# A twelve-sublayer decoder on one core: the delta-rule layer's join, its decay weighting, the latent copy order and one table of decays

## What is computed

```python
scores = jnp.einsum('bhsr,bhlr->bhsl', q_r, k_r)
attn = jax.nn.softmax(scores, axis=-1)
ctx_c = jnp.einsum('bhsl,bld->bhsd', attn, kv_rope)
```

```python
fused_qkv = jax.nn.silu(conv_out)          # causal convolution, 4 taps, over 4096 channels
def step(Sm, inp):
    q_t, k_t, v_t, b_t, a_t = inp
    Sm = Sm * a_t[..., None, None]
    kv = jnp.einsum('bhk,bhkv->bhv', k_t, Sm)
    u = (v_t - kv) * b_t[..., None]
    Sm = Sm + k_t[..., None] * u[:, :, None, :]
    o = jnp.einsum('bhk,bhkv->bhv', q_t, Sm)
    return (Sm, o)
```

## Time and profile before

| | |
|---|---|
| median of 3 runs | 2896.03 us (2892.81 to 2896.42) |
| the profiled execution: own time | 2889.24 us |
| its span | 2887.4 us |
| PE busy | 2364.2 us (82%) |
| DVE busy | 1698.7 us (59%) |
| ACT busy | 1015.2 us (35%) |
| POOL busy | 769.9 us (27%) |

### The profile page before, as it was taken

One profiled execution on the slowest core, in us unless ns is written; L12 is line 12 of the kernel. 1 busy time (PEld: TensorE's weight loads), 2 busy tenths in 40 slices (PEclk: granted clock), 3 DMA queues, 4 the chain that ended last, 5 costly groups with the idle time before them and its releaser, 6 DMA issues. The chain is left out here.

```text
span 2887.4 us, 38148 instructions
## 1 busy us (share of the span) xinstructions
PE 2364.2 (82%) x14562; PEld 1587.5 (55%) x14562; DVE 1698.7 (59%) x3527; ACT 1015.2 (35%) x2336; POOL 769.9 (27%) x573
## 2 busy tenths in 40 slices
PE   6797453348999988878889797889998888999899
PEld 4555322114345555657768586745558665555555
DVE  5435986893445652496969687436656753656311
ACT  3132021651035541135444353435552132555210
POOL 1130001000048862110101010028880000888222
PEclk8689555559999999987979797899999958999999
DMA  1000001002000010220101010210001003000411
GB/s 36 19 21 23 0 0 20 1 23 88 0 1 1 1 51 9 107 57 16 44 16 44 16 45 16 51 52 1 1 1 44 21 6 97 1 1 1 121 38 40
DMA packets 100526, 81.77 MB, mean 28 GB/s; under 512 B 52704, under 2 KB 91857, under 8 KB 99770
## 3 DMA queue, kind: packets, MB, share of 16 engines
q1 hardware_dynamic: 99321, 77.89, 9.5%
q0 software_dynamic: 1024, 1.45, 0.2%
HBM read 73.58 MB, written 5.35 MB: 27 GB/s over the span
## 5 line engine op out<-in xcount | busy, mean ns | idle before, releaser
L2032 POOL TENSOR_SCALAR work<-work,small 128x512 f32<-128x512 f32 x384 | 594.3, 1566 | 706.6 <-DVE small L1967 705.3
L2010 ACT ACTIVATE work<-psum,small 128x512 f32<-128x512 f32 x384 | 260.6, 683 | 254.6 <-DVE small L1962 254.6
L1962 DVE TENSOR_REDUCE small<-psum 128x2 f32<-128x1024 f32 x192 | 234.7, 1224 | 176.0 <-PE psum L1912 176.0
L1922 PEld LDWEIGHTS psum<-consts,work 128*128 128x128 f32 x1536 | 165.5, 141 | 114.0 <-issue 101.8
L1912 PE MATMUL psum<-keysT,arena_a 64*128 64x512 f32 x768 | 219.2, 649 | 8.9 <-ACT work L2010 6.0
L1934 PE MATMUL psum<-work,keys 128*64 128x256 f32 x1536 | 187.0, 384 | 36.6 <-issue 34.2
L1922 PE MATMUL psum<-consts,work 128*128 128x128 f32 x1536 | 211.4, 281 | 3.6 <-DVE work L1973 2.6
L1934 PEld LDWEIGHTS psum<-work,keys 128*64 128x64 f32 x1536 | 120.0, 136 | 136.5 <-issue 110.5
L2864 PE MATMUL psum<-xnT,arena_a 128*128 128x256 f32 x512 | 137.4, 423 | 25.8 <-DVE arena_b L3284 23.8
L1973 DVE COPY work<-psum 128x512 f32<-128x512 f32 x192 | 130.9, 682 | 19.7 <-PE psum L1922 19.5
L2017 ACT ACTIVATE work<-psum 128x512 f32<-128x512 f32 x192 | 114.4, 596 | 71.5 <-PE psum L1922 71.5
(11 more groups left out here) (585 smaller groups left out, 4777.6 us busy)
## 6 DMA issues: line engine op xcount, KB each, us to landing
arena_b<-alpha_rows SPq DMA_DIRECT2D x16, 512.0 KB, 5.7
arena_a<-in_L_xattn_Wo SPq DMA_DIRECT2D x3, 2048.0 KB, 13.6
arena_a<-in_L_xattn_Wq SPq DMA_DIRECT2D x3, 2048.0 KB, 13.7
arena_a<-in_L_xattn_w_kc_q SPq DMA_DIRECT2D x3, 1536.0 KB, 12.8
arena_a<-in_L_attn_w_qkv SPq DMA_DIRECT2D x1, 4096.0 KB
arena_a<-in_L_xattn_W_qr SPq DMA_DIRECT2D x3, 768.0 KB
arena_b<-in_L_ffn_w_fc SPq DMA_DIRECT2D x1, 2048.0 KB
arena_b<-in_L_ffn_w_proj SPq DMA_DIRECT2D x1, 2048.0 KB
```

Source lines behind the costliest of these rows:

```text
L1922: mm = nc.tensor.transpose(ps[:, 4 + j, c * P:(c + 1) * P], probs[u % NPB][:, j, c * P:(c + 1) * P], k.c["ident"])
L1962: nc.vector.tensor_reduce(top[:, 2 * u:2 * u + 2], ps[:, u % 2 * 2:u % 2 * 2 + 2, :], AX.X, ALU.max, negate=True).then_inc(*maxed.up())
L2010: nc.scalar.activation(probs[u % NPB][:, j, :], ps[:, u % 2 * 2 + j, :], ACT.Exp, bias=top[:, i:i + 1], accum_out=total[:, i:i + 1]).then_ ...
L2032: nc.gpsimd.tensor_scalar(probs[u % NPB][:, j, :], probs[u % NPB][:, j, :], total[:, i:i + 1], None, ALU.mult).then_inc(*scaled.up())
```

## The change

It has four parts.

1. In the delta stage the last two value tiles, 14 and 15, are no longer convolved ahead of `turn_blocks` but inside the join: each ahead of one of the two `z1d` copies on DVE. They get a place of their own, `late` (the space of `X`), and tile 15 a bank of its own; their transpositions stand after `close_first` and after `second_level(0)` on PE, their silu and keep between the join's copies on ACT. The join's PSUM banks are packed into 0, 1, 6 and 7 (`join_bank`), and the waits for the kept values move from `close_first` to the products that read them.
2. For g = 2 and 3 the weighting in `lower` is split: ACT writes the key products times `gn` (`weigh_keys`, eight instructions for each g), DVE multiplies all four heads by the decays in one instruction. `lower(b, 3)` comes after `convolve(b, 4)`. ACT's root of the key norms comes after both.
3. In the latent stages ACT copies first and takes the exponentials second in even steps; odd steps stay as they were.
4. In `l0_attn` the exponential is that of half of the argument, and two of the three squarings go.

```diff
-            k.link(act, nc.scalar.activation(powers, arg, ACT.Exp, scale=0.125), "act")
+            k.link(act, nc.scalar.activation(powers, arg, ACT.Exp, scale=0.5), "act")
...
-            k.link(dve, nc.vector.tensor_tensor(powers, powers, powers, ALU.mult), "dve")
-            k.link(dve, nc.vector.tensor_tensor(powers, powers, powers, ALU.mult), "dve")
             dve.wait_ge(*low.at(1))
...
             for s in range(U + LAG):
+                if s % 2 == 0 and 0 <= s - LAG < U:
+                    keep(s - LAG)
                 if s < U:
                     exps(s)
-                if 0 <= s - LAG < U:
+                if s % 2 == 1 and 0 <= s - LAG < U:
                     keep(s - LAG)
...
+    late = over[:, 3072:4096].rearrange("p (n j s) -> p n j s", n=2, j=2)
...
+        if n < 8:
+            return qkT[:, 2 * pair(n):2 * pair(n) + 2, :]
+        return late[:, n - 14] if n >= 14 else vT[:, (n + 2) % 4]
+    def bank_of(n):
+        return 3 if n == 15 else n % 3
+    def join_bank(g):
+        return g if g < 2 else 4 + g
...
-                    pool.wait_ge(*vturned.at(8 * b + 6 + 2 * r))
+                    pool.wait_ge(*vturned.at(8 * b + 4 + 2 * r))
...
-                if n >= 3:
+                if n == 15:
+                    pe.wait_ge(*normed.at(2 * b + 2))
+                elif n >= 3:
                     pe.wait_ge(*conved.at(16 * b + n - 2))
...
-                for n in range(10, 16):
+                for n in range(10, 14):
                     turn_values(b, n)
                     if n < 13:
                         project(b, n + 3)
...
                 close_first(b, 1)
-                for g in range(5):
+                turn_values(b, 14)
+                second_level(b, 0)
+                turn_values(b, 15)
+                for g in range(1, 5):
                     second_level(b, g)
...
+            def weigh_keys(b, g):
+                act.wait_ge(*kkd.at(4 * b + g + 1))
+                if g == 2:
+                    act.wait_ge(*negated.at(b + 1))
+                    if b >= 1:
+                        act.wait_ge(*u1d.at(4 * b))
+                for j in range(2):
+                    for h in range(4 * g + 2 * j, 4 * g + 2 * j + 2):
+                        for c in range(2):
+                            last = nc.scalar.activation(inv[:, h, c * P:(c + 1) * P],
+                                                        ps[:, 4 + g, (2 * j + c) * P:(2 * j + c + 1) * P],
+                                                        ACT.Copy, scale=gn[:, c, h:h + 1])
+                last.then_inc(*weighed.up())
...
                 silu(b, 3)
+                weigh_keys(b, 2)
                 first_tap(b, 4)
-                act.wait_ge(*normed.at(2 * b + 1))
+                weigh_keys(b, 3)
...
             def lower(b, g):
+                if g >= 2:
+                    dve.wait_ge(*weighed.at(2 * b + g - 1))
+                    dve.wait_ge(*scanned.at(8 * b + 2 * g + 2))
+                    nc.vector.tensor_tensor(four(inv, g), four(inv, g), four(decay, g), ALU.mult).then_inc(*lmade.up())
+                    return
...
-                for g in range(4):
+                for g in range(3):
                     lower(b, g)
-                for n in range(4, 8):
+                convolve(b, 4)
+                lower(b, 3)
+                for n in range(5, 8):
                     convolve(b, n)
...
-                for n in range(10, 16):
+                for n in range(10, 14):
                     convolve(b, n)
 
                 turn_blocks(b, 0)
                 turn_blocks(b, 1)
                 for r in range(2):
+                    convolve(b, 14 + r)
                     dve.wait_ge(*z1d.at(2 * b + r + 1))
```

More of the change, by code:

```diff
@@ L2800, in dest @@
     def dest(n):
-        return qkT[:, 2 * pair(n):2 * pair(n) + 2, :] if n < 8 else vT[:, n % 4]
+        if n < 8:
[5 more added lines that the diff above has]
+        return g if g < 2 else 4 + g
     def four(t, g):
```

63 lines of the change are left out of this document (39 added, 24 removed).

## The result

The changed kernel takes 2825.68 us (median of 4 runs, 2822.46 to 2830.59), beside 2895.59 us for the kernel before on the same chip (4 runs, 2892.81 to 2896.42). The ratio is 0.9762, with a 95% interval of 0.9745 to 0.9779: 69 us less, between 64 and 74. The profiled execution took 2822.46 us, and its span is 2820.6 us. The forecast was 2829 us.

A forecast was written before the change was run, and what follows sets the result against it. PE bounds the latent stages, a chain over DVE and PE the delta stage. 39 us latent plus 4 x 6.9 us delta, 67 us off the 2896.0 us median, gave 2829 us, range 2820 to 2847 us.

The forecast's parts named there:

- Part 3, 39 us: Latent stages: with the copy first, PE's 87 waits of 0.45 us before `over_keys` go, 39 us.
- The slack: Latent stages: even-step exponentials start 0.35 us later, with 3 us of slack before the scores two steps on.
- POOL, next in line: Latent stages: POOL has 6.19 us of work in a pair, against 6.92 us; PE stays the bound.
- Part 1, 4.0 us a batch: Delta join: `close_first(1)` gains 5.1 us, less 0.9 and 0.2 for PE's transposes, 4.0 us a batch.
- that for POOL's clearing: Delta join: POOL's clearing keeps its distance to the transposes of tile 13; 0.3 us allowed.
- Part 2, 2.9 us a batch: Delta weighting: DVE saves 1.9 us net, plus 1.0 of the stop before the last `attend`, 2.9 us a batch.
- tile 4's earlier place: Delta, before the solve: tile 4 convolved some 2.9 us earlier starts PE's chain sooner, so 1.0 of the 1.15 us stop goes.
- Part 4, nothing: First layer: dropping two squarings gains nothing; DVE's idle time before its copy becomes 9.4 us instead of 4.24.
- The sum: Whole kernel: 39 + 4 x (4.0 + 2.9) = 66.6, say 67 us.
- PE's granted clock is 0.50, that is 1.2 GHz, throughout: Delta join: PE's clock stays at 1.2 GHz, even when busy for all of 6.00 us.
- PE at 0.50 in the join: Sign for part 1 in the delta join; the prediction is wrong if the clock rises there.
- The rival with the join at 2.4 GHz: Delta join straight after the projections runs at full clock: 8.4 us a batch, 34 us in all, 2795 us; chance 0.06.

The follow-up runs named there:

- The kernel with later tiles: The changed kernel with tile 14 convolved behind both first-level copies, tile 15 behind the first second-level copy; ratio 0.9682 to the kernel before.
- added products: The changed kernel with ten unused products of 128x128 by 512 columns in TensorE's waits of each join; ratio 0.9737 to the kernel before.

## Why the prediction was right

- *Part 3, 39 us.* 87 waits of 0.45 us were the right price: 3 x 13.3 = 39.9 us in the trace, and 39.9 us measured with that part alone, where the interval (35 to 45) makes so close a match chance. The slack was there too: a pause of 1.94 us in front of the exponentials leaves the pair at 6.91 us. POOL, next in line, stands still for 0.73 us in each pair.
- *Part 1, 4.0 us a batch.* The stretch from the solve to the second-level copy is 4.03 us shorter. Of the allowances, that for POOL's clearing was used (a stop of 0.25 us). In batch 1 0.3 us come back behind that copy: 0.12 in the second level, where I had put tile 15's transposes at 0.2, and 0.17 behind the join, unforecast. So 3.7 us are left. The terms inside held too: `close_first(1)` starts 5.1 us earlier, counted from the last step of the solve (22.95 instead of 28.05 us), as forecast, and tile 14's transposes cost 1.04 us ahead of the second level, where I had 0.9.
- *Part 2, 2.9 us a batch.* 3.10 us: the multiplications cost 1.13 us, as taken from the squaring, ScalarE's second group 2.23 us, tile 5's tap came 0.9 us early instead of 0.4, and the stop of 1.15 us went whole, where I had taken 1.0 of it. As to why it went: I named tile 4's earlier place. It gives TensorE's chain 1.13 us more cover, which alone would nearly have done it. Undone, it brings back only 0.45 us, since that chain is by then 0.70 us shorter than before; the granted clock was low for 3.4 us at its start instead of 6.8, which my sum didn't have. The join part isn't the reason, since alone it leaves a stop of 1.34 us.
- *Part 4, nothing.* 0.9995 with that part alone; the idle time is 9.46 us, forecast 9.4.
- *The sum.* 66.6 us forecast, 69 measured (64 to 74). The profiled executions differ by 66.8.
- *The step that failed, without a price.* "PE's granted clock is 0.50, that is 1.2 GHz, throughout", and with it "PE at 0.50 in the join" as the sign to look for. The row behind it began where the small products of before began, at 1478, and there it was true. In the changed kernel `join_first` begins 1.2 us behind the end of the last projection (1449.86 to 1451.08; before, 6.4 us, 1471.24 to 1477.60), and runs at 1.00 to its end. It takes 4.34 us instead of 7.04, and that gained nothing: VectorE, with tile 14 in front of the copy, came to it 7.1 us behind its first transposition, where 6.9 and an allowance of 0.3 were forecast. I wrote that the prediction would be wrong if the clock rose in the join. It was up in the first part of it, and the number held all the same, because TensorE was not what was waited for there. The kernel with later tiles shows that: with the copies first, the same stretch is 3.5 us shorter. As far as the clock goes the number was luck: by my own sign the prediction was wrong.
- *The rival with the join at 2.4 GHz.* Coming straight from the projections gave the join the full clock for its first 4.7 us and not for the rest. Held up by added products, the clock takes 3.7 us off a batch net of what they cost, not 8.4, and 2.4 of them behind the join, which the rival's price did not count. What it would give without the added products isn't shown.

## What to carry to other kernels

A wait of a few tenths of a microsecond that recurs in each step of a full engine is worth its count, and the price is read from two starts of the same instruction, with and without the wait; that price was right to 1 us of 40. Where work is moved into an engine's waits, put it behind the copies that another engine waits for, not ahead of them: the same two tiles gave 16 us in the one place and 23 us more in the other, up to 11 of which came with a clock that rose earlier behind the join. And a clock seen at 0.50 over one stretch need not hold for the stretch beside it: look at what the engine does up to the point where the changed code will begin.

## What the hardware showed unexpectedly

- Small products of 32x32 and 64x64 fill TensorE's time in the profile (6.00 of 6.00 us) with a granted clock of 0.50. With ten products of 128x128 by 512 columns among them it was 1.00 for the whole join, and TensorE was busy for 8.00 of 8.00 us there as well.
- The fall of the clock at one place moves work elsewhere: the same code had a stop of 2.68 us before the last `attend` in one batch and none in another of the same execution; the products that it waits for took 1.91 us at 0.50 in the one and 1.05 us at 1.00 in the other.
- A pause of 1.94 us in 6.91 us on ScalarE was free in the latent stages, though GpSimd, which works on ScalarE's results, is busy for 6.19 us of the same pair.
